# Later places for the transposition of the probabilities and the context products in a fused attention and feed-forward kernel

## What is computed

```python
x = x + tanh(g_xattn) * c            # q = layernorm(x); a = q @ keys.T
                                     # e = softmax(a);   c = e @ keys
x = x + tanh(g_ffn) * y              # z = layernorm(x); y = z @ W.T + bias
                                     # W = mean(|weight|, row) * sign(weight)
```

## Time and profile before

| | |
|---|---|
| median of 2 runs | 1260.21 us |
| the two runs | 1255.38 and 1265.04 us |
| span of the profiled execution | 1256.9 us |
| own time of the profiled execution | not given beside its span |
| busy: PE, DVE, ACT, POOL | 1095.5, 1015.0, 372.4, 243.1 us |
| mean granted TensorE clock, share of full | 0.959 |

### The profile page before, as it was taken

One profiled execution on the slowest core, in us unless ns is written; L12 is line 12 of the kernel. 1 busy time (PEld: TensorE's weight loads), 2 busy tenths in 40 slices (PEclk: granted clock), 3 DMA queues, 4 the chain that ended last, 5 costly groups with the idle time before them and its releaser, 6 DMA issues.

```text
span 1256.9 us, 15376 instructions
## 1 busy us (share of the span) xinstructions
PE 1095.5 (87%) x5776; PEld 542.3 (43%) x5776; DVE 1015.0 (81%) x1258; ACT 372.4 (30%) x470; POOL 243.1 (19%) x304
## 2 busy tenths in 40 slices
PE   2478978789999999999999999999999999999998
PEld 1354643334444444444444444444444444444443
DVE  5786788887888888888888889898888888898632
ACT  3655633222223323322223322333122332333100
POOL 1121022220121222212121222221112122222100
PEclk9878998988999999999999999999999999999999
DMA  8789756254665446445675447554765546554231
GB/s 267 196 196 263 199 104 161 54 109 111 161 158 134 107 96 149 119 113 134 150 167 134 114 107 162 107 122 115 167 141 134 129 111 144 113 117 124 57 59 67
DMA packets 68782, 168.72 MB, mean 134 GB/s; under 512 B 6480, under 2 KB 24912, under 8 KB 59472
## 3 DMA queue, kind: packets, MB, share of 16 engines
q1 hardware_dynamic: 68080, 165.18, 54.7%
q0 software_dynamic: 672, 3.15, 0.8%
HBM read 96.47 MB, written 36.70 MB: 106 GB/s over the span
## 4 chain that ended last, share of the span: by engine, by line
PE 31%; DMA 21%; DVE 20%; ACT 9%; issue 8%; SPq 5%; POOL 4%; ACTq 0%; DVEq 0%
PE y_ps L1096 25%; DMA xs<-xn 20%; DVE xn L701 11%; ACT xn L526 5%; SPq L296 4%; PE c_ps L1088 4%; DVE xr L754 2%; DVE st L759 2%; POOL r L441 2%; ACT x1t L541 2%; POOL ve L439 1%; DMA wstage<-n_L_ffn_weight_real_dram 1%; ACT ex L545 1%; PE setup_ps L1043 1%; DVE qt L721 1%
## 5 line engine op out<-in xcount | busy, mean ns | idle before, releaser
L1096 PE MATMUL y_ps<-wsign,x1t 128*128 128x512 f16 x4096 | 948.6, 388 | 3.6 <-ACT wsign L557 2.4
L1096 PEld LDWEIGHTS y_ps<-wsign,x1t 128*128 128x128 f16 x4096 | 406.4, 100 | 492.8 <-issue 43.0
L701 DVE STREAM_TRANSPOSE xn<-xs 128x1024 f32<-128x1024 f32 x128 | 259.7, 2090 | 61.5 <-DMA xs<-xn 56.0
L439 POOL TENSOR_TENSOR ve<-mv,eps 128x1 f32<-128x1 f32 x64 | 29.2, 457 | 824.3 <-DVE mv L684 527.3
L773 DVE TENSOR_TENSOR xr<-ytmp,xr 128x512 f32<-128x512 f32 x128 | 172.6, 1348 | 3.2
L541 ACT ACTIVATE x1t<-xn 128x2048 f16<-128x2048 f32 x32 | 61.1, 1909 | 350.8 <-DVE xn L701 350.8
L455 POOL TENSOR_TENSOR xr<-xr,bias_b 128x2048 f32<-128x2048 f32 x32 | 144.9, 4527 | 72.9 <-ACT xn L526 68.1
L754 DVE SCALAR_TENSOR_TENSOR xr<-c_ps,coef,xr 128x512 f32<-128x512 f32 x128 | 95.2, 744 | 37.0 <-PE c_ps L1088 36.6
L765 DVE TENSOR_TENSOR ytmp<-y_ps,alpha_b 128x512 f32<-128x512 f32 x128 | 87.8, 686 | 43.7 <-PE y_ps L1096 39.8
L526 ACT ACTIVATE xn<-xr,nm,r 128x2048 f32<-128x2048 f32 x32 | 67.1, 2098 | 123.3 <-POOL nm L445 123.3
L518 ACT ACTIVATE xs<-xs,spread 128x512 f32<-128x512 f32 x128 | 93.8, 803 | 5.7 <-DMA xs<-in_x_dram 2.7
(11 more groups left out here) (70 smaller groups left out, 402.5 us busy)
## 6 DMA issues: line engine op xcount, KB each, us to landing
xr<-in_x_dram SPq DMA_DIRECT2D x32, 1024.0 KB, 5.1
xs<-in_x_dram SPq DMA_DIRECT2D x128, 256.0 KB, 6.6
xs<-xn SPq DMA_DIRECT2D x128, 256.0 KB, 6.9
out_dram<-xr SPq DMA_DIRECT2D x31, 1024.0 KB, 3.9
wstage<-n_L_ffn_weight_real_dram SPq DMA_DIRECT2D x32, 512.0 KB, 8.3
kd_cur<-kd_dram SPq DMA_DIRECT2D x12, 512.0 KB, 5.6
kt_cur<-kt_dram SPq DMA_DIRECT2D x6, 512.0 KB, 8.0
xr<-in_ctx_dram SPq DMA_DIRECT2D x4, 512.0 KB, 6.8
```

What stands on the lines that cost most here:

```text
L701: last = nc.vector.transpose(dst[:, D // 2 * h:D // 2 * (h + 1)].rearrange("p (k i c) -> p k c i", k=8, c=4), src[:, :].rearrange("p (c h ...
L1096: last = nc.tensor.matmul(y_ps[:, bank, :], x1t[:, slot, part, P * k:P * (k + 1)], wsign[:, k, chunk(n)], start=(k == 0 and part == 0), st ...
```

## The change

```diff
-    SCORES_AT, PT_AT, C_AT, SPREAD_AT = 2, 4, {6: 0, 7: 1, 8: 2, 9: 3}, 8
+    SCORES_AT, PT_AT, C_AT, SPREAD_AT = 2, 6, {7: 0, 8: 1, 9: 2, 10: 3}, 11
```

## The result

| | before | after |
|---|---|---|
| median | 1260.21 us | 1336.38 us |
| the two runs | 1255.38, 1265.04 | 1335.7, 1337.06 |
| span of the profiled execution | 1256.9 | 1335.3 (own time 1337.06) |
| mean granted TensorE clock | 0.959 | 0.942 |

The change makes the kernel slower: the ratio is 1.058, with a 95% interval of 1.046 to 1.071. The prediction said 1324 us with a range of 1288 to 1345.

What follows compares the result with a forecast made beforehand. Bound: a ring across engines and DMA, 34.28 us a step, TensorE's hole being slack. Span 1256.9 + 54 (25 steps x 2.15) + 10 (clock) = 1321, plus 3.3 for the median: 1324 us, range 1288 to 1345.

Steps and rivals of the forecast that it cites:

- The hole: TensorE's wait ahead of the transposition, 2.87 us; said to move to block 8, at 3.2 us, waiting for scale_y(t, 0).
- P: Start of the transposition of the probabilities on TensorE in a step; the prediction gives other times in us after it.
- the 2.15: normalise2's delay per step on ScalarE, in us: 1.28 from the late block 8 and 0.87 from the spread.
- The ring: Chain from transposition through product 3, normalise2, DMA and turn_x1 to the next transposition: 34.28 us, forecast 36.43.
- The clock: TensorE falling from 2.4 to 1.2 GHz behind the hole: 20 of 25 steps, +10 us, ends -23 and +18.
- The ends: Steps outside 4 to 28: step 3 at +1.2 us, step 29 at -1.0, together nothing.
- the forecast's own case: Whole kernel at 1308 to 1335 us, by 14 to 25 low-clock steps and 2.0 to 2.3 us a step; chance 63%.
- the 1190: Rival: the change does what it seems meant to, block 8 not waiting, 1.93 us less per step: 1190 us; 4%.
- The transposing copies: Rival: GpSimd's add_bias also holds VectorE's transposing copies (turn_q), 107 us more, 1431 us; 3%.
- the case at 1356: Rival: holes at the transposition, blocks 8, 12 and 0 give a second clock fall in most steps: 1356 us; 7%.
- the recovered clock: Rival: the move's cost stands but shorter holes keep TensorE at 2.4 GHz throughout, +31 us: 1291 us; 10%.
- the hidden spread: Rival: the later spread costs nothing, only block 8's 1.28 us a step counts, +42 us: 1302 us; 8%.

Runs made afterwards that it cites:

- The experiment with the early scale_y: Changed kernel with scale_y(t, 0) ahead of low_x1 and the four statistics in VectorE's queue, norm_mean1 behind add_y(t, 0): 1231.5 us, ratio 0.976.
- the filled kernel: Changed kernel plus 14 unread matmuls of 512 columns ahead of block 8's wait: 1291.2 us, ratio 1.024.
- The two experiments on the spread: Changed kernel with the spread back behind block 9: 1316.8 us; kernel before with only the spread moved, from behind block 8 to behind 11: 1342.3 us.
- The two experiments with filled holes: Unread matmuls added: 14 ahead of block 8's wait in the changed kernel, 1291.2 us; 12 ahead of the transposition in the kernel before, 1238.9 us.
- chunk 0 out of the way: Changed kernel, spread behind block 10, finish_y(t, 0) in VectorE's wait for the exponential, norm_mean1 behind the first addition, place_factors behind the second: 1196.0 us, ratio 0.945.

## Why the prediction was right

**The hole is moved, not removed.** Predicted: under 1 us at the transposition, some 3 us ahead of block 8. Measured: 0.3 and 3.13 by the record, in a step of the same shape throughout. Block 8 at P + 5.44, measured P + 5.52; in the filled kernel P + 5.43. The experiment with the early scale_y shows the cause.

**The spread behind block 11 holds normalise2.** Predicted P + 17.17 with the clock up; measured P + 18.85 with 1.69 lost in blocks 8 and 9, so P + 17.16. turn_q's new wait for ScalarE was to be 2.3 and is 2.07. The two experiments on the spread show this part. They also show what the prediction's split of the 2.15 into 1.28 and 0.87 did not say: alone, the spread costs as much as both together.

**The ring.** Predicted +2.15 a step and 36.43 in all; measured +2.07 and, in the filled kernel, 36.42. 25 steps make +51.6 where I had 54.

**The clock is the term that was mis-sized.** I took 20 of 25 steps at 1.62, so +10, with +18 as the upper end. It was 24 steps at an average of 1.85, so +21.8, above that end. Not only did the clock fall in nearly every step, in five of them the fall was longer and cost 2.9 us (block 8 took 3.6 in those). The two experiments with filled holes show that this is the clock: the slow blocks vanish, with 45 and 20 us.

**The ends.** I had step 3 and step 29 at nothing together; they and what stood ahead of them came to +5.0. Of this 1.6 us were there at the transposition of step 2, where the two kernels are still the same. That is chance: in the twelve profiles this point lies between 224.5 and 227.4. From there to the transposition of step 4 it was +2.3 (70.88 for 68.60), 0.3 of it ahead of the transposition of step 3, which now stands behind block 6; 1.2 were predicted for step 3. In step 29 product 3 came at P + 8.98 as predicted (9.0), but the gain of 1.0 didn't reach the end: the hole ahead of block 8 of step 30 grew from 1.20 to 2.60 and the clock fell behind it, so the last 192 matmuls took 43.30 instead of 41.61. That makes +1.1.

So 1324 became 1336 by the clock (+12) and the ends (+5), less the ring (-2) and less what the median lies above the span (1.1 here, 3.3 before). That the total is only 12 us off owes a little to errors of both signs. The range of the forecast's own case, 1308 to 1335, ended 1 us below the measured time.

**The rivals.** Block 8 does wait, so the 1190 did not come, but such a time was not out of reach: with chunk 0 out of the way and the spread behind block 10 the changed places give 1196. The transposing copies are not held by GpSimd: turn_q from 775.00 and add_bias from 777.03 lie beside each other for 2 us, and turn_q takes 4.07. A second fall of the clock in a step, the case at 1356, does not show in any of the 25 steps, although small holes stand ahead of blocks 12 and 0. The cases of the recovered clock and of the hidden spread are what the filled kernel (1291) and the spread behind block 9 (1317) show; the first was priced right at 1291. The second was priced at 1302, too low by both its terms: the clock was +16.5 and not +10, and the ring +1.57 a step and not +1.28, mostly since behind block 9 the spread stands ahead of product 3.

## What to carry to other kernels

Where several engines and DMAs form a ring, a hole in the busiest engine can be slack and not the bound. Before work is moved past it, go down that engine's queue and ask of every wait that is now reached earlier how much cover it had (here 0.74 us for a move of 3.9). A reordering on one engine is worth what the orders of the others allow: nearly the same places (the spread stood behind block 11 and then behind block 10) cost 6% with one VectorE order and gave 5.5% with another, which puts the needed step into a wait that was there anyway. A hole in TensorE's stream has a second price in the clock, which filler matmuls into an unused bank can show and even win back.

## What the runs showed of the hardware

- Holes of 3.2 us ahead of block 8 (3.04 to 3.43 by the record) let the clock fall in 24 of 24 steps, the one of 2.84 in step 4 did not; in the kernel before holes of 2.65 to 3.04 did so in 14 of 25. The length of the hole does not decide it alone: in the kernel before, the holes with and without a fall have the same lengths, and with the spread behind block 9 one hole of 3.14 (step 25) had no fall behind it. Steps with holes of at most 1.6 us show none. A fall cost mostly 1.3 to 1.7 us, in the longer cases 2.8 to 2.9.
- 14 matmuls of work that nobody reads, in each of 26 steps, made a kernel 45 us faster (1336.4 to 1291.2); 12 of them made the other 20 us faster.
- An operation of VectorE with two operands from SBUF (low_x1, 2.23 us; add_y, 0.64) holds even GpSimd operations on a single element per row: the same one takes 2.11 us beside low_x1, 0.52 beside add_y and 0.19 beside neither. The transposing copies of VectorE don't: beside turn_q, in the kernel with both instructions for chunk 0 in the wait, GpSimd's later small steps took 0.55, 0.19 and 0.19, as without it.
- Two operands are not needed for a hold. While the kernel before fills its pipeline, VectorE's tensor_scalar on the exponentials (line 742, one operand from SBUF, 0.20 us otherwise) took 3.63 us and 4.17 us beside an add_bias of 4.5, and ended with it.
